# A two-layer decoder with two mixtures of experts on one core: the order of the first mixture's work, written out by hand

## The chip, the cores and the metric

One core of one Trainium2 chip runs the whole program in one launch. The metric is the device time of that launch in microseconds (us). The core has TensorE (matmul, with weight loads of its own), VectorE, ScalarE, GpSimd, and SyncE, which only issues DMAs here. Each engine has one queue that it works in order; the engines meet by semaphores alone.

## The reference, cut to what matters

The program is a decoder of six blocks over x (8 sequences of 112 tokens, 256 channels), each of them a residual block with a layer norm behind it: a linear attention, a cross attention with an MLP, a mixture of 8 experts, a second causal attention, a second cross attention, and a mixture of 4 experts. The change concerns the third block alone:

```python
capacity = max(1, int(CF * N / E))            # 896 tokens, E = 8, CF = 1.25: 140 slots for each expert
disp = zeros((E, capacity + 1, D)).at[se, pos].set(xf[st])[:, :capacity]
g = jnp.einsum('ecd,edf->ecf', disp, wg)      # D = 256, F = 1024
u = jnp.einsum('ecd,edf->ecf', disp, wu)
eo = jnp.einsum('ecf,efd->ecd', jax.nn.silu(g) * u, wd)
```

A router picks two experts for each token; a token beyond an expert's 140 slots is dropped. Every expert runs over all of its 140 slots.

## The kernel before, in words

The program is cut into seven stages (0 to 6); the stage numbered 2 is the first mixture of experts. Within a stage the builder first makes a plan, a list of units such as `("up", e, f)`, and then each engine's function (`tensor_s2`, `scalar_s2`, `vector_s2`, `gpsimd_s2`, `sync_s2`, L1275 to L1539) walks the same list and issues its own part of each unit. So the order of the plan is the order of every queue. `step(...)` tells of each unit which semaphore marks it sets, which PSUM bank it takes and who frees it, and a nominal cost. `place(unit)` appends a unit. `weave(...)` takes several generators in turn and places what they yield; `until(...)` holds a generator back until named units are placed, and `rest(ns)` until units of so much nominal cost are placed.

The units of stage 2, for expert e:

- `ein`: ScalarE issues the DMA that brings the expert's 140 rows (140 KB) from DRAM (L1347). For the first it waits for the last of the 16 scatters with which GpSimd puts the tokens into their slots (L1520, eight after each of the two `slot2`); later ones wait for the transposes of two experts before.
- `einT`, `einS`: TensorE turns the rows (four transposes, L1305); ScalarE writes the float16 high half, VectorE the low half (L1355, L1488). All products of the experts are three float16 products, high x high, high x low and low x high.
- `split(e, j, half)`, j = 0, 1, 2 for wg, wu, wd: one half of one weight (128 x 1024) is copied from float32 to float16 times 64 by ScalarE (L943), and VectorE computes the low rest from raw and high (L948). It waits for the weight's load, and, since the float16 buffers are two and the expert two before had the same one, for that expert's last up-product (wg, wu) or its down-products (wd).
- `load(e, j)`: SyncE issues the 1 MB load of expert e's weight j (L1533). There is one raw buffer for each of the three weights, so it waits for both halves of the split of expert e-1's weight j.
- `up(e, f)`, f = 0 to 7: 12 matmuls of 128 x 128 with 140 columns, gate then up. ScalarE computes silu (L1362), VectorE multiplies (L1495). `hid(e, f)`, for two f at once: ScalarE copies the product to float16 (L1369), VectorE subtracts (L1500). It waits for the gate of f+1.
- `down0(e)`, `down1(e)`: 24 matmuls with 256 columns each, for the two halves of the slots (L344 through `mm`, as all products). They need all of `hid` and of wd. VectorE then copies the result out (L1508) and SyncE stores it (L1537).

The plan before comes from four generators, `s2_down`, `s2_up`, `s2_in` and `s2_split`. What they place for a middle expert, here expert 1 with what stands around it, is:

```
up.0.7 split.2.0.0 hid.0.6 split.2.0.1 load.3.0 split.2.1.0 split.2.1.1 load.3.1
down0.0 einT.1 down1.0 einS.1 split.2.2.0 up.1.0 ein.2 split.2.2.1 up.1.1 load.3.2
up.1.2 hid.1.0 up.1.3 up.1.4 hid.1.2 up.1.5 up.1.6 hid.1.4 up.1.7 split.3.0.0 hid.1.6
```

At the head of the experts' part stand `ein.0`, the six splits of expert 1 (each pair with the load of expert 2 behind it), `einT.0`, `einS.0` and then `up.0.0`; expert 0's weights were split in stage 1. The last expert's ups are woven with the downs of the one before. The plan up to `slots2` (router, ranks, scatters) is the same before and after the change. `mx2` is a ring of the eight PSUM banks; up frees its bank with the gate, down with the copy out, einT with the low half.

Of the kernel before, what the change touches and what calls it, by code (L numbers as in the profile page):

```python
# [30 lines left out]
E0, F0, CAP = 8, 1024, int(1.25 * T_ / 8)  # L31
SLOTS = E0 * CAP
HC = CAP // 2
FT = F0 // P
# [107 lines left out]
def program(nc, a, out):  # L142
    with ExitStack() as ctx:
        build(nc, ctx, a, out)


def build(nc, ctx, a, out):
# [3 lines left out]
    def results(name, by=1):  # L151
        return Results(ctx.enter_context(nc.semaphore(name)), by)
# [10 lines left out]
    def parse(text):  # L163
        out = []
        for word in text.split(","):
            if word.strip():
                engine, name = word.split()
                out += [(engines[engine[0]], name)] if name[0] != "+" else \
                    [(engines[engine[0]], None)] * int(name)
        return out  # L170

    def step(what, marks="", bank=None, freed="", cost=0.0):

        steps[what] = (parse(marks), bank, parse(freed), cost)

    def place(unit):
        what, *at = unit
        marks, bank, freed, cost = steps[what]
        for result, name in marks:
            result.plan((name, *at) if name else None)  # L180
        if bank:
            rings[bank.replace("#", str(at[0])) if "#" in bank else bank].take(unit, *((r, (n, *at)) for r, n in freed))
        plans[-1].append(unit)
        placed.add(unit)
        spent[0] += cost
# [3 lines left out]
    def weave(*streams):  # L189
        live, passed = list(streams), 0  # L190
        while live:
            for stream in list(live):
                units = next(stream, "end")
                passed = 0 if units else passed + 1
                hurry[0] = passed >= len(live)
                assert passed <= 3 * len(live), "every stream waits for another"
                if units == "end":
                    live.remove(stream)
                    continue
                for unit in units or ():  # L200
                    place(unit)

    def until(*units):
        while any(u not in placed for u in units):
            yield None

    def rest(ns):
        end = spent[0] + ns
        yield None
        while spent[0] < end and not hurry[0]:  # L210
            yield None

    def follow(work, items):
        for i in items:
            yield from work(i)
# [10 lines left out]
    def end_stage():  # L226
        fences.append([r.planned() for r in (T, A, V, G)])
# [44 lines left out]
    eout = nc.dram_tensor("expert_out", [SLOTS, D], F32)  # L272
# [65 lines left out]
    L_eout = [results(f"dma_e_out{i}", 16) for i in range(2)]  # L338
# [33 lines left out]
    REST, REST_POWER, POWER_NS = 1500.0, 1500.0, 180.0  # L372
# [531 lines left out]
    def split_units(e, j):  # L904
        for half in range(2):
            yield [("split", e, j, half)]
# [294 lines left out]
    step("down0", "", "mx2", "V eo", 2600)  # L1201
    step("down1", "T down, V eo", cost=2600)
    step("load")

    def count_passes(b, hf):


        cut = min(max(b - 4 * hf, 0), 4) * N
        out = [(lo, hi, op) for lo, hi, op in ((0, cut, ALU.is_ge), (cut, HALF, ALU.is_gt)) if hi > lo]
        first = len(count_passes(b, 0)) if hf else 0  # L1210
        return [(*p, first + n) for n, p in enumerate(out)]
# [15 lines left out]
            L_put.plan(("put", k, b))  # L1227
    place(("slots2",))

    def s2_in(e):  # L1230
        if e >= 2:
            yield from until(("einT", e - 2))
        yield [("ein", e)]
        L_in[e % 2].plan(("ein", e))
        yield from rest(3 * REST)
        if e >= 2:
            yield from until(("up", e - 2, FT - 1))
        yield [("einT", e)]
        yield [("einS", e)]

    def s2_up(e):
        yield from until(("einS", e), ("split", e, 0, 1), ("split", e, 1, 1))
        if e >= 2:
            yield from until(("down1", e - 2))
        for f in range(FT):
            if f % 2 == 0:
                rings["silu2"].take((e, f), (V, ("hid", e, f)))
            units = [("up", e, f)]
            if f % 2 == 0 and f:
                units.append(("hid", e, f - 2))  # L1250
            yield units
        yield [("hid", e, FT - 2)]

    def s2_down(e):
        yield from until(("up", e, FT - 1), ("hid", e, FT - 2), ("split", e, 2, 1))
        yield from rest(2 * REST)
        yield [("down0", e)]
        L_eout[e % 2].plan(("eout", e))
        yield [("down1", e)]

    def s2_split(e):
        for j in range(3):
            if e >= 2:
                yield from until(("up", e - 2, FT - 1) if j < 2 else ("down1", e - 2))
            yield from split_units(e, j)
            if e + 1 < E0:
                place(("load", e + 1, j))

    weave(*(follow(w, range(E0)) for w in (s2_down, s2_up, s2_in)), follow(s2_split, range(1, E0)))
    end_stage()  # L1270

    def wide(t):
# [1673 lines left out]
```

## Time and profile before

| what | us |
|---|---|
| median of 3 runs (1519.33 to 1522.53) | 1519.48 |
| the profiled execution's own time | 1514.58 |
| its span | 1512.8 |
| TensorE matmul busy in it | 1147.1 (76%) |
| VectorE busy | 724.9 (48%) |
| ScalarE busy | 601.4 (40%) |
| GpSimd busy | 293.4 (19%) |

The busy times are sums over engines that work beside each other, so they don't add up to the span. The span is from the first to the last instruction of the profiled execution. The part of the experts lies between 406 and 556 us of it. A row of the timeline gives start, duration, engine, line, operation, the tiles written and read, and the count of merged instructions; in square brackets stands how long the engine had been idle before, and what ended that.

### The profile page before, as it was taken

The page shows a single profiled execution, that of the slowest core. Times are in us where ns is not written, and L with a number is a line of the kernel's source. Part 1 is how long each engine was busy: PE and PEld are TensorE (multiplying, and loading weights), DVE is VectorE, ACT ScalarE, POOL GpSimd, SP SyncE. Part 2 cuts the span into 40 slices and gives each one's busy share as a digit, 9 for nine tenths or more (in the row PEclk, how much of TensorE's full clock was granted, in tenths as well). Part 3 has the DMA queues.
Part 4 walks back from the last instruction along what each step waited for, and adds up shares of the span by engine and source line. Part 5 has one row for each costly group of instructions (what it writes and reads, how often), then busy time and mean ns, then how long its engine had stood idle before and what let it go on. Part 6 is the DMA issues. An engine that isn't in the chain of part 4 may idle for free.

```text
span 1512.8 us, 20695 instructions
## 1 busy us (share of the span) xinstructions
PE 1147.1 (76%) x8320; PEld 810.4 (54%) x8320; DVE 724.9 (48%) x1676; ACT 601.4 (40%) x1404; POOL 293.4 (19%) x308
## 2 busy tenths in 40 slices
PE   7987687875177755867769878878888577768996
PEld 4665465653077653545555555555556345554764
DVE  3323576216656626645433645545555355444403
ACT  4311275420145512433324533444445245447452
POOL 3311133100400024111111011001000604313353
PEclk9867699666589886788889999999999778776998
DMA  8400244004255322000005000000000000000000
GB/s 278 87 0 26 56 91 93 12 0 153 96 191 188 129 102 69 1 0 1 0 1 221 1 11 9 4 11 1 1 1 1 1 0 1 1 1 1 1 2 25
DMA packets 32752, 70.62 MB, mean 47 GB/s; under 512 B 8256, under 2 KB 22560, under 8 KB 28448
## 3 DMA queue, kind: packets, MB, share of 16 engines
q1 hardware_dynamic: 29888, 64.48, 13.9%
q0 software_dynamic: 1536, 3.67, 0.8%
q8 instruction: 65, 1.06, 0.3%
q10 hardware_dynamic: 1232, 1.15, 0.3%
q14 instruction: 31, 0.25, 0.1%
HBM read 60.19 MB, written 9.04 MB: 46 GB/s over the span
## 4 chain that ended last, share of the span: by engine, by line
PE 47%; DVE 27%; ACT 16%; POOL 4%; issue 3%; DMA 2%; SPq 0%; ACTq 0%; DVEq 0%; POOLq 0%
PE psum L344 39%; ACT s_p L2047 4%; DVE s_p L2099 3%; DVE s_k L2068 2%; POOL rs L2467 2%; DVE s_max L1115 2%; ACT sc L2347 2%; PE psum L1003 2%; DVE s_max L2088 2%; PE psum L975 1%; ACT s_k L2020 1%; DVE s_pT L2080 1%; DVE junk L1448 1%; DVE s_q L1767 1%; DVE k L2411 1%
## 5 line engine op out<-in xcount | busy, mean ns | idle before, releaser
L496 POOL TENSOR_TENSOR rstd<-meanvar,minus_half 112x1 f32<-112x1 f32 x40 | 23.2, 579 | 508.0 <-DVE meanvar L482 507.9
L2047 ACT ACTIVATE s_p<-psum,s_max 112x375 f32<-112x375 f32 x128 | 72.1, 568 | 103.6 <-DVE s_max L2088 103.6
L344 PE MATMUL psum<-ctx,Wk 128*128 128x375 f16 x320 | 64.2, 332 | 26.0 <-DVE s_k L2068 11.8
L2068 DVE SCALAR_TENSOR_TENSOR s_k<-psum,s_k 128x375 f16<-128x375 f32 x64 | 34.0, 546 | 96.8 <-ACT s_k L2020 96.8
L1115 DVE TENSOR_REDUCE s_max<-psum 112x2 f32<-112x750 f32 x64 | 59.9, 936 | 39.2 <-PE psum L975 38.4
L344 PE MATMUL psum<-wd,hid 128*70 128x256 f16 x384 | 55.8, 314 | 21.6 <-DVE hid L1500 21.6
L344 PE MATMUL psum<-x_ch,w_Wq 128*128 128x224 f32 x192 | 55.7, 421 | 14.8 <-DVE s_k L2068 8.7
L344 PE MATMUL psum<-Wv,ctx 128*125 128x512 f16 x240 | 63.3, 395 | 2.9 <-ACT s_v L2027 1.4
L456 PE MATMUL psum<-ident,x_tok 112*128 112x112 f32 x80 | 18.2, 325 | 61.0 <-DVE x_tok L491 57.6
L2088 DVE TENSOR_REDUCE s_max<-psum 112x1 f32<-112x375 f32 x128 | 63.6, 538 | 0.0
L344 PEld LDWEIGHTS psum<-wd,hid 128*70 128x70 f16 x384 | 48.7, 132 | 26.2 <-DVE hid L1500 22.9
L1067 ACT ACTIVATE s_pT<-psum 125x672 f32<-125x672 f32 x64 | 46.7, 730 | 38.7 <-PE psum L991 37.4
L1987 PE MATMUL psum<-ident,s_p 112*125 112x112 f32 x384 | 56.1, 278 | 5.0 <-DVE s_p L2099 5.0
L2777 POOL TENSOR_TENSOR hidden<-raw,hidden 128x448 f16<-128x448 f32 x44 | 46.7, 1061 | 64.2 <-ACT hidden L2660 62.5
L344 PEld LDWEIGHTS psum<-ctx,Wk 128*128 128x128 f16 x320 | 27.2, 99 | 57.8 <-DVE s_k L2068 18.6
L2347 ACT ACTIVATE sc<-psum,mx 112x112 f32<-112x112 f32 x128 | 33.9, 362 | 58.0 <-DVE mx L2420 58.0
L1987 PEld LDWEIGHTS psum<-ident,s_p 112*125 112x125 f32 x384 | 49.6, 188 | 13.1 <-DVE s_p L2099 10.0
L1998 PE MATMUL psum<-s_pT,s_v 125*64 125x112 f32 x768 | 53.2, 276 | 0.6 <-ACT s_attT L2055 0.6
L473 DVE TENSOR_TENSOR res<-res,psum 112x256 f32<-112x256 f32 x24 | 10.1, 421 | 91.0 <-PE psum L344 91.0
L344 PEld LDWEIGHTS psum<-x_ch,w_Wq 128*128 128x128 f32 x192 | 38.9, 221 | 27.2 <-DVE s_k L2068 14.5
L1979 PE MATMUL psum<-s_k,s_q 64*112 64x375 f16 x384 | 44.0, 334 | 11.8 <-ACT s_p L2047 11.7
L975 PE MATMUL psum<-s_kd,s_qd 48*112 48x375 f16 x128 | 27.2, 420 | 33.5 <-DVE s_max L1115 25.7
(352 smaller groups left out, 2818.1 us busy)
## 6 DMA issues: line engine op xcount, KB each, us to landing
raw_wg<-in_wg SPq DMA_DIRECT2D x8, 1024.0 KB, 4.9
raw_wu<-in_wu SPq DMA_DIRECT2D x8, 1024.0 KB, 6.4
raw_wd<-in_wd SPq DMA_DIRECT2D x8, 1024.0 KB, 4.9
ctx_raw<-in_ctxT SPq DMA_DIRECT2D x16, 375.0 KB, 3.5
s_kd<-k_halves SPq DMA_DIRECT2D x48, 93.8 KB, 3.8
k_halves<-s_k SPq DMA_DIRECT2D x8, 375.0 KB, 3.5
w_Wv<-in_Wv SPq DMA_DIRECT2D x2, 1024.0 KB, 9.9
w_Wo<-in_Wo SPq DMA_DIRECT2D x2, 1024.0 KB, 11.9
```

Source lines behind the costliest of these rows:

```text
L344: ins = TE.matmul(bank, left, right, start=i == 0, stop=last)
L1067: SC.activation(rings["pT1"][n], rings["t1"][unit][0:SCH, :, 0:NCH * N], ACT.Exp, scale=0.25).then_inc(*A.up("exp1", n))
L1115: VE.tensor_reduce(s1_max[b % 2][:, 2 * p:2 * p + 2], rings["s1"][unit][0:N, :, 0:S], X, ALU.max, negate=True).then_inc(*V.up("max1", n))
L1979: ins = TE.matmul(rings["s4"][(n, j)][0:N, 0:S], q[rows, p, u, cols(b % 2)], k[rows, p, v, :], start=i == 0, stop=i == 2)
L1987: ins = TE.transpose(rings["t4"][unit][0:SCH, c * N:(c + 1) * N], p[:, c * SCH:(c + 1) * SCH], ident[0:N, 0:N])
L1998: ins = TE.matmul(rings["o4"][n // 4][64 * j:64 * j + 64, p % 4 * N:(p % 4 + 1) * N], s4_v[p // 4][:, c, 2 * (p % 4) + j, :], rings["pT4"] ...
L2047: SC.activation(rings["p4"][2 * n + j], rings["s4"][(n, j)][0:N, 0:S], ACT.Exp, bias=s4_max[b % 2][:, h:h + 1], accum_out=s4_sum[b % 2][:, ...
L2068: VE.scalar_tensor_tensor(s4_k[b % 2][:, t, 1, :], rings["misc4"][unit][:, 0:S], 1 / WSCALE, s4_k[b % 2][:, t, 0, :], ALU.mult, ALU.subtra ...
L2088: VE.tensor_reduce(s4_max[b % 2][:, h:h + 1], rings["s4"][(n, j)][0:N, 0:S], X, ALU.max, negate=True).then_inc(*V.up(name, n))
L2099: VE.tensor_scalar(t, t, sums[:, j:j + 1], None, ALU.mult).then_inc(*V.up(name, n))
L2347: SC.activation(s[:, j, :], bank[:, j, :], ACT.Exp, bias=mx5[b % 2][:, 4 * g + j:4 * g + j + 1]).then_inc(*(A.up("exp5", *at) if j == 3 el ...
L2777: GP.tensor_tensor(dst[:, 1, f, :], raw_, dst[:, 0, f, :], ALU.subtract).then_inc(*G.up("ll", *at))
```

## The change: what it does

The four generators and their weave go. In their place the plan is written out in two loops. Expert 1's six splits are placed first, ahead of `ein.0`; the loads of expert 2 stay behind each pair. Then come `ein.0`, `ein.1`, `einT.0`, `einS.0`, `ein.2`, and for each expert its eight ups. Within them stand, at fixed f: the halves of the next expert's splits (`SPLITS`: wg behind f = 0 and 1, wu behind 3 and 4, wd behind 5 and 6), each second half followed by the load for the expert after; behind f = 2 the two downs of the expert before, in a row; behind f = 4 `einT` and `einS` of the next expert and the `ein` of the third from here. The last expert's downs stand at the end. Units, engines' functions, buffers and waits are as they were. For a middle expert e the order is now:

```
up.e.0 split.e+1.0.0 up.e.1 split.e+1.0.1 load.e+2.0 up.e.2 hid.e.0 down0.e-1 down1.e-1
up.e.3 split.e+1.1.0 up.e.4 hid.e.2 split.e+1.1.1 load.e+2.1 einT.e+1 einS.e+1 ein.e+3
up.e.5 split.e+1.2.0 up.e.6 hid.e.4 split.e+1.2.1 load.e+2.2 up.e.7 hid.e.6
```

```diff
--- before.py
+++ after.py
@@ -1201,6 +1201,7 @@
     step("down0", "", "mx2", "V eo", 2600)
     step("down1", "T down, V eo", cost=2600)
     step("load")
+    SPLITS = {0: (0, 0), 1: (0, 1), 3: (1, 0), 4: (1, 1), 5: (2, 0), 6: (2, 1)}
 
     def count_passes(b, hf):
 
@@ -1227,46 +1228,45 @@
             L_put.plan(("put", k, b))
     place(("slots2",))
 
-    def s2_in(e):
-        if e >= 2:
-            yield from until(("einT", e - 2))
-        yield [("ein", e)]
+    def expert_in(e):
+        place(("ein", e))
         L_in[e % 2].plan(("ein", e))
-        yield from rest(3 * REST)
-        if e >= 2:
-            yield from until(("up", e - 2, FT - 1))
-        yield [("einT", e)]
-        yield [("einS", e)]
-
-    def s2_up(e):
-        yield from until(("einS", e), ("split", e, 0, 1), ("split", e, 1, 1))
-        if e >= 2:
-            yield from until(("down1", e - 2))
+
+    def split_expert(e, j, half):
+        place(("split", e, j, half))
+        if half and e + 1 < E0:
+            place(("load", e + 1, j))
+
+    for j in range(3):
+        for half in range(2):
+            split_expert(1, j, half)
+    expert_in(0)
+    expert_in(1)
+    place(("einT", 0))
+    place(("einS", 0))
+    expert_in(2)
+    for e in range(E0):
         for f in range(FT):
             if f % 2 == 0:
                 rings["silu2"].take((e, f), (V, ("hid", e, f)))
-            units = [("up", e, f)]
+            place(("up", e, f))
             if f % 2 == 0 and f:
-                units.append(("hid", e, f - 2))
-            yield units
-        yield [("hid", e, FT - 2)]
-
-    def s2_down(e):
-        yield from until(("up", e, FT - 1), ("hid", e, FT - 2), ("split", e, 2, 1))
-        yield from rest(2 * REST)
-        yield [("down0", e)]
-        L_eout[e % 2].plan(("eout", e))
-        yield [("down1", e)]
-
-    def s2_split(e):
-        for j in range(3):
-            if e >= 2:
-                yield from until(("up", e - 2, FT - 1) if j < 2 else ("down1", e - 2))
-            yield from split_units(e, j)
-            if e + 1 < E0:
-                place(("load", e + 1, j))
-
-    weave(*(follow(w, range(E0)) for w in (s2_down, s2_up, s2_in)), follow(s2_split, range(1, E0)))
+                place(("hid", e, f - 2))
+            if f == 2 and e:
+                place(("down0", e - 1))
+                L_eout[(e - 1) % 2].plan(("eout", e - 1))
+                place(("down1", e - 1))
+            if 0 < e < E0 - 1 and f in SPLITS:
+                split_expert(e + 1, *SPLITS[f])
+            if f == 4 and e + 1 < E0:
+                place(("einT", e + 1))
+                place(("einS", e + 1))
+                if e + 3 < E0:
+                    expert_in(e + 3)
+        place(("hid", e, FT - 2))
+    place(("down0", E0 - 1))
+    L_eout[(E0 - 1) % 2].plan(("eout", E0 - 1))
+    place(("down1", E0 - 1))
     end_stage()
 
     def wide(t):
```

## Rows read from the trace of the kernel before

**Rows 1.** The page: span of the profiled execution

```profile
span 1512.8 us, 20695 instructions
```

**Rows 2.** Windows: stretch, length, busy PE, PEld, DVE, ACT, POOL, granted clock, DMA

```profile
415.50:426.07 10.57, 7.63 (x96) 7.45 (x96) 5.29 (x14) 5.88 (x15) 0.00 (x0) 0.82 0.44 176
426.07:517.83 91.76, 68.42 (x741) 63.42 (x741) 58.05 (x101) 47.26 (x96) 0.00 (x0) 0.87 0.54 188
517.83:549.66 31.83, 26.36 (x296) 25.31 (x296) 15.59 (x33) 11.26 (x30) 0.00 (x0) 0.89 0.06 15
```

**Rows 3.** Timeline, experts 1 and 2: start, duration, engine, line, operation

```profile
434.47 0.53 PE L344 MATMUL psum<-e_inT,wg 128*128 128x140 f16 x6 [1.23 <-ACT wd L943]
...
435.40 0.29 ACT L1362 ACTIVATE silu<-psum 128x140 f32<-128x140 f32 x1 [1.06 <-PE psum L344]
...
435.77 1.06 ACT L943 ACTIVATE wd<-raw_wd 128x1024 f16<-128x1024 f32 x1
...
436.86 1.23 DVE L948 SCALAR_TENSOR_TENSOR wd<-raw_wd,wd 128x1024 f16<-128x1024 f32 x1 [0.83 <-ACT wd L943]
...
439.17 0.51 DVE L1495 SCALAR_TENSOR_TENSOR silu<-psum,silu 128x140 f32<-128x140 f32 x2
...
441.00 0.27 ACT L1362 ACTIVATE silu<-psum 128x140 f32<-128x140 f32 x1
...
441.17 1.05 ACT L943 ACTIVATE wg<-raw_wg 128x1024 f16<-128x1024 f32 x1
...
443.39 0.44 DVE L1500 TENSOR_TENSOR hid<-silu,hid 128x280 f16<-128x280 f32 x1
443.75 1.22 DVE L948 SCALAR_TENSOR_TENSOR wg<-raw_wg,wg 128x1024 f16<-128x1024 f32 x1
...
443.89 5.33 PE L344 MATMUL psum<-wd,hid 128*70 128x256 f16 x24 [3.40 <-DVE hid L1500]
```

**Rows 4.** Timeline of PE: the first down-product of expert 3

```profile
481.07 4.11 PE L344 MATMUL psum<-wd,hid 128*70 128x256 f16 x24 [3.39 <-DVE hid L1500]
```

**Rows 5.** Timeline, experts 6 and 7

```profile
535.26 0.86 PE L344 MATMUL psum<-e_inT,wg 128*128 128x140 f16 x6 [2.51 <-DVE e_inT L1488]
...
539.66 2.78 PE L344 MATMUL psum<-wd,hid 128*70 128x256 f16 x24
...
542.28 0.53 PE L344 MATMUL psum<-e_inT,wg 128*128 128x140 f16 x6
...
545.63 0.53 PE L344 MATMUL psum<-e_inT,wg 128*128 128x140 f16 x6
...
547.10 0.53 PE L344 MATMUL psum<-e_inT,wg 128*128 128x140 f16 x6
...
548.35 0.30 DVE L1495 SCALAR_TENSOR_TENSOR silu<-psum,silu 128x140 f32<-128x140 f32 x1
548.69 0.44 ACT L1369 ACTIVATE hid<-silu 128x280 f16<-128x280 f32 x1 [0.37 <-DVE silu L1495]
...
549.66 5.43 PE L344 MATMUL psum<-wd,hid 128*70 128x256 f16 x48 [1.67 <-DVE hid L1500]
```

**Rows 6.** Chain that ended last, start of the experts: start, duration, what

```profile
403.78 2.55 DMA dispatched<-x_tok,put_i
406.36 0.59 ACTq L1347
...
412.72 2.27 DVE wd L948 x2
...
415.50 7.65 PE psum L344 x96
```

**Rows 7.** Timeline: expert 0's transposes

```profile
408.55 0.73 PE L1305 MATMUL psum<-ident,e_in 70*128 70x70 f32 x4 [20.98 <-DMA e_in<-dispatched]
```

**Rows 8.** The page, DMA issues: count, KB each, median us to landing

```profile
raw_wg<-in_wg SPq DMA_DIRECT2D x8, 1024.0 KB, 4.9
raw_wu<-in_wu SPq DMA_DIRECT2D x8, 1024.0 KB, 6.4
```

## The prediction, made blind

> **What bounds the kernel now.** I read the page first: the span [rows 1] and, in its slices, where the change can act at all. The diff touches only the stage of the first mixture's experts, so the sum is made there. The windows of that stage give its size [rows 2]: 10.57 us for the first expert's up-products, 91.76 us from the first down-product to the sixth (five periods of 18.35 us, one for each expert), 31.83 us for the last two. In the five periods TensorE is busy 68.42 of 91.76, VectorE 58.05, ScalarE 47.26: no engine is full, so it is a chain of waits, and the timeline shows it [rows 3]. Before each down0 TensorE waits 3.40 us for the low half of hid. That half is the last of its expert, and it stands on VectorE behind the first split of the weights that the expert after the next will use; the split's high half on ScalarE stands ahead of the last hid copy too (wg on ScalarE at 441.17, the low half of hid on VectorE only at 443.39). During the two downs that follow, ScalarE and VectorE are mostly idle, having run out of placed work; then wd's first split (released by the down) stands ahead of the first gate, and TensorE waits 1.23 us more. The third thing to see is the price of the wait itself: down0 after it takes 5.33 us for 24 matmuls at 443.89 and 4.11 at 481.07 [rows 3, 4], where the same 24 take 2.78 at 539.66 [rows 5], with no wait ahead. That is the lower of the two clock levels (1.2 GHz beside 2.4) for the most part of it. Six down0 run so, between those two durations; the middle is 4.7, or 1.9 over the warm one.
>
> The chain at the start [rows 6]: the last put lands at 406.33, ScalarE issues ein.0, and only then are expert 1's six halves copied, until 414.99, though their loads were issued at the head of the stage. The transposes of expert 0 are done at 409.3 [rows 7], but the copy of e_inT that they need stands on VectorE behind the six. up.0.0 starts at 415.50.
>
> **The start.** Expert 1's splits are now placed ahead of ein.0. ScalarE does them while VectorE still counts; VectorE does its six lows after slots2, while GpSimd puts. Six lows at 1.135 (2.27 for two [rows 6]) are 6.8 us and fit ahead of the last landing. The chain becomes: ein.0 at 406.36, transposes 408.55 to 409.28, high copy of e_inT about 0.4 and low 0.44 with 0.1 between, up.0.0 at 410.25: 5.25 earlier. New on this stretch are three 1 MB loads for expert 2, issued by SP after each pair, so some 10 us sooner and beside the puts. A load that has another beside it takes 6.4 against 4.9 [rows 8], 1.3 times. The last put (2.55) and ein.0 (2.2) stretched likewise cost 1.4; with GpSimd's own issue slightly slower I take 1.5. Bounds: 0 and 5.2 (puts and load doubled). Start: 3.75 gained.
>
> "GPSIMD Engine Reference" of the Trainium skill (Key points) says that GpSimd shares its SBUF interfaces with VectorE and contends with its instructions of two SBUF inputs, which the low copies are. No row read here has a put beside such a copy; if GpSimd stood still for all six the start would be 6.8 later and the whole gain 14.6 instead of 21.4.
>
> **Expert 0.** Its up-products take 7.65 with their tail (cold start included), 7.5 to the next start [rows 6]. Then TensorE no longer stops: up.1.0 to 1.2 follow at 0.735 for each f (545.63 to 547.10 is two [rows 5]), and the last hid half of expert 0 comes meanwhile, about 9.3 after up.0.0 (no splits stand ahead in e = 0). down0.0 starts at 9.7 against 10.57: 0.9 gained.
>
> **The period.** I walk the new order e by e, from down0(e-1) to down0(e), taking at each head of a queue whichever comes last:
> - Both downs warm, 2.62 each to the next start (539.66 to 542.28 [rows 5]): 5.24. In this time ScalarE and VectorE do the silu, gate and both halves of split (e+1, wg): 2 x 1.05 and 2 x 1.135, hidden.
> - up(e,3) is queued behind the downs; its silu starts 0.93 after it (434.47 to 435.40 [rows 3]). VectorE stands at the copy of e_out, which waits for the same downs, so it loses nothing to it.
> - silu to the high half of (e+1, wu): 0.17; high to low: 1.09 (435.77 to 436.86).
> - From here VectorE has work in a row: four lows at 1.135 = 4.54, gates 4, 5, 6 at 0.21 = 0.63 (0.51 for two), hid 0.36 twice (443.39 to 443.75) and the low of e_inT, taken as 0.43: 6.32. ScalarE's share of this (three highs, three silus, two hids, e_inT, one DMA issue) is about 5 us and stays ahead; each hid copy waits for the gate before, while a low keeps VectorE busy.
> - gate 7 to its hid copy 0.34, hid copy to down0 0.97 (548.35, 548.69, 549.66 [rows 5]).
> Sum 5.24 + 0.93 + 0.17 + 1.09 + 6.32 + 0.34 + 0.97 = 15.06, against 18.35. What hides the splits is the down pair and the fact that up 5 to 7 need only a bank of eight; if ScalarE fell behind, each low would wait as the second wd split does now (0.83 idle at 436.86 [rows 3]). Five periods: 16.45 gained.
>
> **The last two experts.** A sixth period of 15.06, then e = 7 with no splits: downs 5.24, f 3 to 6 at 0.735 = 2.94, and 2.56 from f 7 to the last down (547.10 to 549.66 [rows 5]): 10.74. Together 25.80 against 31.83: 6.03 gained.
>
> **The loads.** Each is issued after its pair: wg at about 4 us into a period, wu at 11, wd at 15, and wanted no sooner than 10 us later, for 4.9 to 6.4 us [rows 8]. Hidden. The three compete with one e_out and one ein of 140 KB. SP's queue holds the e_out store between wg's and wu's load, in the order of VectorE's work, so nothing waits behind it that is ready.
>
> Sum with a full clock: 3.75 + 0.90 + 16.45 + 6.03 = 27.1.
>
> **The clock.** In the walk TensorE is idle twice in each period. up 7 is issued 4.0 after up 3 (five f, four transposes of half of 0.73), at 9.3; up(e+1,0) needs the low of e_inT, at 10.8: about 1.4 idle. Three f later, at 13.1, it waits for hid until 15.06: 1.95 idle. Waits of 1.23 and 1.67 left the matmuls at full speed, 2.51 and 3.40 did not [rows 3, 5]. 1.95 lies between, nearer to 1.67, but it has the other wait shortly before. So I take three falls in six at 1.9: 5.7 lost. Bounds: 0, and 11.4 for six.
>
> Forecast: 27.1 - 5.7 = 21.4 us. The profiled execution is 1514.58 (span 1512.8), 4.9 below the median of the runs, 1519.48; the difference lies outside the argument, and I subtract from the median: 1498.
>
> **Rivals.**
> 1. The clock holds throughout: 27.1 gained, 1492.4. For it: 1.67 held. Against: two waits close together.
> 2. It falls before every down0: 15.7, 1503.8. For it: all six down0 after hid are slow now. Against: those waits were 3.40.
> 3. The splits aren't hidden in the up-products: in each of the four late halves VectorE waits 0.83 for ScalarE, 3.3 in a period, which is then 18.4 again. Left are 3.75 + 0.9 + (31.83 - 29.14) = 7.3: 1512. For it: each silu now stands behind a 1.05 us copy, and hid copies chain the two engines. Against: ScalarE has some 5 us of work in a stretch of 7.4.
> 4. Slower: TensorE never gets back to full speed, since it isn't busy in one piece any more. Place: the down pair, now on the path with nothing to cover it. Downs then cost 10.3 in place of 5.24 and the first up 0.7 more: a period of 20.8. It decides from 3.3 us of loss in a period. 5 x 2.45 + 8.4 (last two, 40.2) + 4.8 (expert 0's ups and three more, 11 at 1.4) - 3.75 = 22 slower: 1541. Against: TensorE is busy 11.6 of 15, more than the 68.42 of 91.76 of now, which is granted 0.87 on average [rows 2].
> 5. The change doesn't do what it says: the queues' order is the same where it counts, or another resource sets the stage. Within 0.2%: about 1519.5. Against: the waits named are all from the order of two in-order queues.
>
> **Chances.** Forecast 0.40, rival 1 0.24, rival 2 0.16, rival 3 0.12, rival 4 0.04, rival 5 0.04. What a measurement can tell from no change is 0.2%, 3 us: rivals 1 to 3 and the forecast are faster, 0.92; same 0.04; slower 0.04. The range holds the forecast with rivals 1 and 2 and the other bounds of the start: 1489 to 1509.
>
> **What would show it.** up.0.0 at about 411 to 412 instead of 415.5 (the start; below 410 or above 414 is wrong). Distance between down0s of 15 to 17 us; 18 with VectorE waiting for ScalarE in the lows is rival 3. TensorE's wait before down0 at 1.9, before up(e,0) at 1.4; a first down of 2.8 or of 4 to 5 us says whether the clock held. VectorE waiting for e_out's downs once in each period and then busy without a break. Loads all landed before their split. Wrong from the ground: a wait of TensorE for a bank, or silus that come late because ScalarE is full.

## The result, and the profile after

The changed kernel takes 1499.16 us (median of 4 runs, 1492.97 to 1504.21) against 1519.4 (4 runs, 1517.25 to 1522.53): a ratio of 0.9875, 95% interval 0.9832 to 0.9918. Timed again over six runs (experiment 10) it took 1501.28 against 1518.79, 0.9868 (0.9837 to 0.9899). By these ratios it is 19 to 20 us less. 1498 had been forecast.

The runs of one kernel spread by 5 to some 25 us, and much of that lies outside the changed part: the stretch ahead of the second eight puts ended at 395.07 in the trace of before and at 389.06 in that of after (389.1 to 400.2 over all twelve traces), and what lies behind the last down took 963.1 and 969.3. So all that follows is read from three stretches within the stage: from the first put of the second eight to up.0.0, from there to down0.0, and from down0.0 to down0.7. They don't repeat equally well. The third took 100.89 or 100.90 in five traces with the same loop; the first took 21.7 to 22.3 in six traces in which the kernel's start was the changed one; the second moves by some 0.9 with the place at which the clock rises in it.

The windows of after answer to [rows 2]; the columns are the same.

```profile
411.06:420.90 9.84, 9.84 (x136) 9.84 (x137) 4.64 (x14) 5.58 (x16) 0.00 (x0) 0.84 0.10 30
420.90:496.01 75.11, 58.54 (x744) 56.79 (x741) 56.61 (x100) 45.28 (x96) 0.00 (x0) 1.00 0.65 215
496.01:521.79 25.78, 20.80 (x256) 20.26 (x256) 15.85 (x33) 12.08 (x30) 0.00 (x0) 1.00 0.15 50
```

Five periods take 75.11 us where they took 91.76. VectorE and ScalarE do about the same work in both (100 and 101 instructions, 56.61 and 58.05 us; 96 and 96, 45.28 and 47.26 us). TensorE's busy time is 9.88 less, and that is not less work either: it has 744 matmuls where it had 741, and the granted clock is 1.00, not 0.87, from the first down to the last. The rest of the 16.65 us, 6.77, is time in which TensorE no longer stands idle (16.57 in place of 23.34). By this count more than half of what the five periods gained is the clock, and less than half is the waits themselves. That the shorter waits are what kept the clock up is borne out by experiment 5.

The timeline of after around one down shows the chain that is left (to be held against [rows 3]):

```profile
461.83 0.53 PE L344 MATMUL psum<-e_inT,wg 128*128 128x140 f16 x6 [1.55 <-DVE e_inT L1488]
...
463.51 1.22 DVE L948 SCALAR_TENSOR_TENSOR wd<-raw_wd,wd 128x1024 f16<-128x1024 f32 x1
...
464.65 0.30 DVE L1495 SCALAR_TENSOR_TENSOR silu<-psum,silu 128x140 f32<-128x140 f32 x1
464.98 0.44 ACT L1369 ACTIVATE hid<-silu 128x280 f16<-128x280 f32 x1 [1.49 <-DVE silu L1495]
...
465.45 0.45 DVE L1500 TENSOR_TENSOR hid<-silu,hid 128x280 f16<-128x280 f32 x1 [0.50 <-ACT hid L1369]
...
465.95 5.43 PE L344 MATMUL psum<-wd,hid 128*70 128x256 f16 x48 [1.76 <-DVE hid L1500]
...
471.22 0.53 PE L344 MATMUL psum<-e_inT,wg 128*128 128x140 f16 x6
...
471.49 0.69 DVE L1508 TENSOR_SCALAR e_out<-psum 70x512 f32<-70x512 f32 x1 [1.78 <-PE psum L344]
...
472.15 0.29 ACT L1362 ACTIVATE silu<-psum 128x140 f32<-128x140 f32 x1 [3.67 <-PE psum L344]
...
473.42 1.23 DVE L948 SCALAR_TENSOR_TENSOR wu<-raw_wu,wu 128x1024 f16<-128x1024 f32 x1 [0.64 <-ACT wu L943]
```

The wait of 3.40 before the down is 1.76 now, both downs follow each other at full speed (5.43 for 48), and the next down0 starts at 480.98: a period of 15.03. ScalarE is idle for 3.67 us ahead of the fourth silu and VectorE for 1.78 ahead of the e_out copy; this is where the down pair lies bare on the path.

The start looks otherwise than forecast. Here are VectorE, SyncE and GpSimd in the timeline of after, and behind them the last put from issue to release in its chain that ended last:

```profile
388.85 2.35 DVE L948 SCALAR_TENSOR_TENSOR wg<-raw_wg,wg 128x1024 f16<-128x1024 f32 x2
389.06 7.51 POOL L1520 DMA_INDIRECT dispatched<-x_tok,put_i  x1 [3.51 <-DVE w_k L1483]
391.12 2.36 DVE L948 SCALAR_TENSOR_TENSOR wu<-raw_wu,wu 128x1024 f16<-128x1024 f32 x2
391.28 0.33 SPq L1533 DMA_DIRECT2D raw_wg<-in_wg  x1
393.39 2.36 DVE L948 SCALAR_TENSOR_TENSOR wd<-raw_wd,wd 128x1024 f16<-128x1024 f32 x2
...
396.87 0.94 POOL L1520 DMA_INDIRECT dispatched<-x_tok,put_i  x1 [0.30 <-issue]
...
404.37 2.55 DMA dispatched<-x_tok,put_i
```

The first of the eight puts takes 7.51 us in place of 0.94: it starts 0.2 us after VectorE has begun the six low copies and ends 0.8 us after the last of them. The last put is issued 15.31 us after the first, not 8.71. From its issue to up.0.0 it is 6.69 us, where it was 11.72; so the reordering gave the 5.03 us that it was meant to give, and the stopped put took 6.60.

The Trainium skill ("GPSIMD Engine Reference", Key points) says that GpSimd shares its SBUF interfaces with VectorE and contends with its instructions of two SBUF inputs. The trace agrees, and shows how much it came to here: GpSimd finished no put during the six.

### The profile page after: what moved, and what is told of

It reads as the page before. It is cut to its first block, busy times and chain, and to the rows that moved or that the text cites. A ratio compares the mean times of both kernels' runs of the same rounds, so it can differ in the third digit from the quotient of the medians.

```text
span 1491.1 us, 20688 instructions
## 1 busy us (share of the span) xinstructions
PE 1137.2 (76%) x8320; PEld 801.7 (54%) x8320; DVE 723.0 (48%) x1676; ACT 600.1 (40%) x1404; POOL 300.4 (20%) x308
## 3 DMA queue, kind: packets, MB, share of 16 engines
q0 software_dynamic: 1536, 3.67, 0.8%
## 4 chain that ended last, share of the span: by engine, by line
PE 48%; DVE 27%; ACT 15%; POOL 5%; issue 3%; DMA 2%; SPq 0%; DVEq 0%; ACTq 0%; POOLq 0%
PE psum L344 39%; ACT s_p L2047 4%; DVE s_p L2099 3%; DVE s_k L2068 2%; POOL rs L2467 2%; DVE s_max L1115 2%; ACT sc L2347 2%; DVE s_max L2088 2%; PE psum L1003 2%; PE psum L975 2%; ACT s_k L2020 1%; DVE s_pT L2080 1%; DVE junk L1448 1%; DVE s_q L1767 1%; DVE wu L948 1%
## 5 line engine op out<-in xcount | busy, mean ns | idle before, releaser
L1987 PEld LDWEIGHTS psum<-ident,s_p 112*125 112x125 f32 x384 | 49.6, 188 | 13.1 <-DVE s_p L2099 10.0
L344 PE MATMUL psum<-wd,hid 128*70 128x256 f16 x384 | 43.4, 273 | 12.2 <-DVE hid L1500 12.2
L2099 DVE TENSOR_SCALAR s_p<-s_p,s_sum 112x375 f32<-112x375 f32 x128 | 51.3, 443 | 2.3
```

Source lines behind the costliest of these rows:

```text
L344: ins = TE.matmul(bank, left, right, start=i == 0, stop=last)
L1987: ins = TE.transpose(rings["t4"][unit][0:SCH, c * N:(c + 1) * N], p[:, c * SCH:(c + 1) * SCH], ident[0:N, 0:N])
L2099: VE.tensor_scalar(t, t, sums[:, j:j + 1], None, ALU.mult).then_inc(*V.up(name, n))
```

## The experiments

Each is an edit of the changed kernel, except number 4; number 10 is the changed kernel itself. Numbers 1, 5, 6, 7 and 9 were run once each. The three stretches of all of them, in us, read from the starts of the puts (L1520), of the first up and of the downs in each timeline:

| kernel | first put to up.0.0 | to down0.0 | to down0.7 | sum |
|---|---|---|---|---|
| before | 20.43 | 10.57 | 123.59 | 154.59 |
| after | 22.00 | 9.84 | 100.89 | 132.73 |
| 1 loads placed late | 22.29 | 10.18 | 100.90 | 133.37 |
| 2 ein.0 first | 20.43 | 10.46 | 100.89 | 131.78 |
| 3 splits in expert 0 | 15.77 | 14.00 | 100.93 | 130.70 |
| 4 old weave, splits first | 22.00 | 10.99 | 124.02 | 157.01 |
| 5 downs at f = 1 | 22.10 | 10.31 | 113.89 | 146.30 |
| 6 downs at f = 3 | 21.74 | 10.60 | 92.05 | 124.39 |
| 7 downs at f = 4 | 21.72 | 12.36 | 81.31 | 115.39 |
| 8 splits in expert 0, downs late in f = 4 | 15.57 | 14.25 | 81.44 | 111.26 |
| 9 one input | 18.69 | 10.77 | 100.89 | 130.35 |
| 10 changed kernel again | 22.08 | 10.78 | 100.90 | 133.76 |

**1. The loads of expert 2 later in the plan.**

```diff
-        if half and e + 1 < E0:
+        if half and 1 < e < E0 - 1:
             place(("load", e + 1, j))
...
     place(("einS", 0))
+    for j in range(3):
+        place(("load", 2, j))
```

> The changed kernel with the three loads of expert 2 placed behind einS.0 instead of beside the puts. Theory A (VectorE's copies with two SBUF inputs hold GpSimd): the first put of the second eight still lasts about 7.5 us, the time of the six low copies, and the last put is issued 15.3 us after it, as in the changed kernel. Rival B (the 1 MB loads on the same DMA engines hold it): with no load there the put lasts 0.94 us and the eight take 8.7 us, so up.0.0 comes 6.6 us sooner after the first put. The loop is unchanged under both: six periods of 15.0 us.

The put lasted 7.51 us as theory A has it (1498.16 us), but the run doesn't tell the theories apart, since the edit did not move the loads:

```profile
398.27 7.51 POOL L1522 DMA_INDIRECT dispatched<-x_tok,put_i  x1 [3.52 <-DVE w_k L1485]
400.34 2.35 DVE L948 SCALAR_TENSOR_TENSOR wu<-raw_wu,wu 128x1024 f16<-128x1024 f32 x2
400.49 0.33 SPq L1535 DMA_DIRECT2D raw_wg<-in_wg  x1
```

SyncE has nothing else in its queue there and waits only for the pair's two marks; a place further down a plan delays nothing on a queue that is empty up to it. The load still goes out 2.2 us after the put's start. The run settles nothing; experiment 9 takes its place.

**2. ein.0 ahead of the splits, as before.**

```diff
+    expert_in(0)
     for j in range(3):
         for half in range(2):
             split_expert(1, j, half)
-    expert_in(0)
```

> The changed kernel with ein.0 placed ahead of expert 1's six splits, as the kernel before had it; the loop stays as changed. Both theories: puts at 0.94 us each, eight of them in 8.7 us, since the low copies then come after the last put has landed; up.0.0 20.4 us after the first put of the second eight (22.0 in the changed kernel, 20.4 in the kernel before). The time is 1.6 us under the changed kernel's if the start's reordering was a loss, and 5 us over it if it was the gain that the prediction had. Loop: down0.0 to down0.7 100.9 us as in the changed kernel, 22.7 less than before; so some 22 to 23 us faster than the kernel before.

```profile
393.55 0.94 POOL L1520 DMA_INDIRECT dispatched<-x_tok,put_i  x1 [3.54 <-DVE w_k L1483]
```

The puts are 0.94 us each again and up.0.0 comes after 20.43 us, to the hundredth what it was before the change. The loop's 100.89 stays. 1494.29 us (4 runs), a ratio to before of 0.9837 (0.9793 to 0.9881). Against the changed kernel the trace gives 1.57 us less at the start and, with the clock rising later in expert 0's ups, 0.95 less in all; the runs can't tell the two apart. So the rewritten loop is the whole gain, and the new start has no part in it.

**3. Expert 1's splits within expert 0's ups.**

```diff
-    for j in range(3):
-        for half in range(2):
-            split_expert(1, j, half)
     expert_in(0)
...
-            if 0 < e < E0 - 1 and f in SPLITS:
+            if e < E0 - 1 and f in SPLITS:
```

> The changed kernel with expert 1's splits taken out of the head and placed within expert 0's ups, at the same f as for every other expert. Theory A: nothing holds GpSimd, the puts take 8.7 us, and up.0.0 starts 15.2 us after the first of them (22.0 in the changed kernel). Expert 0's ups then carry six splits: down0.0 comes 13.1 us after up.0.0 instead of 9.8. Together 3.5 us faster than the changed kernel. Rival: VectorE and ScalarE are late in expert 0 by more than that (no down pair hides wg's split) and the 6.8 us are given back: no change.

15.77 to up.0.0 and 14.00 to down0.0, against 15.2 and 13.1 expected: 2.0 us less than the changed kernel by the trace, not 3.5, and too little for the runs to tell (1497.57 us, 4 runs; 0.9868 of before, 0.9821 to 0.9914). With no low copy beside them the puts take 0.94 us each. The splits cost 4.2 us in expert 0's ups, where they are no longer hidden, of the 6.2 that the start gains.

**4. The kernel before with the new start alone.**

```diff
-    weave(*(follow(w, range(E0)) for w in (s2_down, s2_up, s2_in)), follow(s2_split, range(1, E0)))
+    for j in range(3):
+        for half in range(2):
+            place(("split", 1, j, half))
+        place(("load", 2, j))
+    weave(*(follow(w, range(E0)) for w in (s2_down, s2_up, s2_in)), follow(s2_split, range(2, E0)))
```

> The kernel before with one part of the change alone: expert 1's six splits (and the loads of expert 2 behind each pair) ahead of ein.0; the weave stays for all the rest. Theory A (low copies hold GpSimd): the first put of the second eight lasts 7.5 us, up.0.0 22.0 us after it instead of 20.4; 1 to 2 us slower than the kernel before, or not to be told from it. The prediction's own term: up.0.0 16.7 us after the first put, 3.75 us faster. Five periods of 18.35 us in both.

```profile
400.20 7.50 POOL L1524 DMA_INDIRECT dispatched<-x_tok,put_i  x1 [3.55 <-DVE w_k L1487]
408.01 0.94 POOL L1524 DMA_INDIRECT dispatched<-x_tok,put_i  x1 [0.30 <-issue]
```

Up.0.0 after 22.00 us, 1.57 later than before; the runs say 1.0037 (1526.2 us, 10 runs; 1.0000 to 1.0073), slower if anything. The term for the start had the wrong sign.

**9. What holds the put.** In the changed kernel the six low copies of expert 1 are replaced by six reductions, each over the same 1024 raw elements and nothing else. The low halves of expert 1's weights are set to zero behind einS.0 (three memsets, left out of the lines below), so that part of the computation is missing. It is placed here because it belongs to the start.

```diff
+        if e == 1:
+            n = src.shape[1]
+            VE.tensor_reduce(hid0[1][:, 0, 2 * j + half, 0:n], src, X, ALU.max).then_inc(*V.up("lo", e, j, half))
+            return
         VE.scalar_tensor_tensor(lo, src, WSCALE, hi, ALU.mult,
                                 ALU.subtract).then_inc(*V.up("lo", e, j, half))
```

> The changed kernel, but VectorE's six low copies for expert 1 are replaced by six reductions over the same raw halves, which read one SBUF tensor of 1024 elements instead of two and take about as long; the lows of expert 1 are set to zero later (so that part of the computation is left out). Theory A (it is the second SBUF input that holds GpSimd): the puts last 0.94 us each although VectorE is as busy beside them; last put issued 8.7 us after the first of the second eight, up.0.0 after 15.4 to 15.8 instead of 22.0. Rival B (VectorE working without a break holds GpSimd, whatever it reads): the first put still lasts as long as the six, 7 us.

VectorE and SyncE first, then GpSimd, then the last put from issue to release:

```profile
394.64 2.34 DVE L950 TENSOR_REDUCE hid<-raw_wg 128x1 f16<-128x1024 f32 x2
396.89 2.34 DVE L950 TENSOR_REDUCE hid<-raw_wu 128x1 f16<-128x1024 f32 x2
397.06 0.33 SPq L1540 DMA_DIRECT2D raw_wg<-in_wg  x1
399.15 2.34 DVE L950 TENSOR_REDUCE hid<-raw_wd 128x4 f16<-128x1024 f32 x2
```

```profile
394.85 0.94 POOL L1527 DMA_INDIRECT dispatched<-x_tok,put_i  x1 [3.54 <-DVE w_k L1487]
396.09 0.94 POOL L1527 DMA_INDIRECT dispatched<-x_tok,put_i  x1 [0.30 <-issue]
397.34 0.94 POOL L1527 DMA_INDIRECT dispatched<-x_tok,put_i  x1 [0.30 <-issue]
```

```profile
403.57 5.78 DMA dispatched<-x_tok,put_i
```

VectorE is as busy (7 us in a row), the loads go out beside the puts at the same distance (2.2 us after the first), and GpSimd issues every put in 0.94 us. So neither the loads nor a busy VectorE hold GpSimd; the low copies do. They differ from the reductions in two ways: they read a second SBUF tensor, and they write 1024 elements where the reduction writes a few. This run doesn't tell which of the two holds GpSimd.

The other half of the expectation failed: up.0.0 came after 18.69 us, not 15.5 (1497.28 us). Without the stop the last put is issued 2.0 us after the last of the three loads, and it takes 5.8 us to its release instead of 2.55. That is the collision which the prediction priced at 1.4 for the put and ein.0 together; here it is 3.2 for the put alone. The loads are the likely cause (in experiment 3, with none of them there, the last put takes 2.56), but no run has the reductions without the loads.

**5. The downs one f earlier.** (`if f == 2 and e:` becomes `if f == 1 and e:`.)

> The changed kernel with the two downs of the expert before behind f = 1 instead of f = 2: TensorE has 0.73 us less to do ahead of them and waits 2.5 us for hid where it waited 1.76. Theory A (a wait of 1.76 is short enough, one of 2.5 is not, as at 535.26 in the kernel before): the clock falls, the first down lasts 4 us or more in most of the six, and the period is 15.8 plus 1.5 to 1.9, about 17.4. Rival B (the clock holds because TensorE is fuller over the whole period): downs of 2.7 us each, a period of 15.8, which is the 0.73 of the up-product that now stands behind the downs and nothing else.

```profile
438.44 5.43 PE L344 MATMUL psum<-wd,hid 128*70 128x256 f16 x48 [2.49 <-DVE hid L1500]
454.20 7.10 PE L344 MATMUL psum<-wd,hid 128*70 128x256 f16 x48 [2.49 <-DVE hid L1500]
471.63 7.10 PE L344 MATMUL psum<-wd,hid 128*70 128x256 f16 x48 [2.49 <-DVE hid L1500]
```

(1507.98 us.) The first wait of 2.49 left the clock at its upper level, five further ones (2.49 and 2.50) did not: 7.10, 7.10, 7.07, 6.91 and 6.82 us for 48 matmuls. Two periods of 15.8 and then four of 17.2 to 17.4: theory A, with its number. 0.73 us of waiting more costs 1.4 to 1.67 us of slow matmuls besides. The wait before the ups is 1.55 as in the changed kernel, so the wait before the down is the only one that grew. Against this stand 37 waits of 1.76 or 1.77 before a down in six executions (after and experiments 1, 2, 3, 9, 10), and behind none of them a slow one.

That holds for this loop and is not a rule on the length of a wait. In a later stage of the kernel before, TensorE waited 1.88 us after a busy stretch at full clock, and half a microsecond after it went on, the clock fell. The windows (columns of [rows 2]) stand behind the row:

```profile
913.36 1.42 PE L344 MATMUL psum<-x_ch,w_Wq 128*128 128x224 f32 x4 [1.88 <-DVE s_k L2068]
...
909.00:911.40 2.40, 2.40 (x17) 1.47 (x16) 2.36 (x7) 0.64 (x2) 0.00 (x0) 1.00 0.00 0
914.30:915.00 0.70, 0.70 (x6) 0.29 (x6) 0.00 (x0) 0.19 (x1) 0.00 (x0) 0.50 0.00 0
```

**6 and 7. The downs later.** (`f == 3` and `f == 4` in the same line.)

> The changed kernel with the downs behind f = 3. Theory A (the period is the downs, then what VectorE has left behind the e_out copy, then gate 7 to hid to down): the first up behind the downs no longer has a silu and a split's high half in front of VectorE, which goes on at once: 5.24 + 0.2 + 0.69 (e_out) + four lows 4.54 + e_inT 0.43 + three gates 0.63 + two hids 0.72 + 0.34 + 0.97 = 13.8 us instead of 15.0. TensorE waits 1.0 before the down. Rival B (ScalarE sets the second half): still 15.0.

> The changed kernel with the downs behind f = 4 (ahead of the second half of wu's split). Theory A: one low, one gate and one hid fewer stand behind the e_out copy: 5.24 + 0.2 + 0.69 + 3.41 + 0.43 + 0.63 + 0.36 + 0.34 + 0.97 = 12.3 us in each period, six of them 16 us less than in the changed kernel. Rival B (TensorE or the banks set it): no less than 13.8.

```profile
454.89 5.43 PE L344 MATMUL psum<-wd,hid 128*70 128x256 f16 x48 [1.03 <-DVE hid L1500]
...
468.57 5.43 PE L344 MATMUL psum<-wd,hid 128*70 128x256 f16 x48 [1.02 <-DVE hid L1500]
```

```profile
453.63 5.43 PE L344 MATMUL psum<-wd,hid 128*70 128x256 f16 x48 [0.29 <-DVE hid L1500]
...
465.66 5.43 PE L344 MATMUL psum<-wd,hid 128*70 128x256 f16 x48 [0.29 <-DVE hid L1500]
```

The first two rows are of experiment 6, the others of experiment 7. The periods are 13.68 and 12.03 us, against 13.8 and 12.3 by the sum. The runs gave 1492.13 and 1480.99 us; the three stretches together are 8.3 and 17.3 us less than in the changed kernel (down0.0 itself, behind one and two further ups, comes 0.8 and 2.5 later). Whatever VectorE can do during the downs must stand ahead of the e_out copy in its queue. From experiment 6 to 7 one low, one gate and one hid went from behind it to ahead of it, 1.70 us of VectorE's work, and 1.65 came off the period.

**8. The edit of experiment 3, and the downs behind all of f = 4.** The lines show what is added; left out are experiment 3's lines and the block `if f == 2 and e:`, which is taken away.

```diff
                 if e + 3 < E0:
                     expert_in(e + 3)
+            if f == 4 and e:
+                place(("down0", e - 1))
+                L_eout[(e - 1) % 2].plan(("eout", e - 1))
+                place(("down1", e - 1))
```

> Two edits together: expert 1's splits within expert 0's ups (2 us gained in an earlier run) and the downs behind everything that f = 4 places (wu's second half, einT, einS). Theory A: behind the e_out copy stand two lows, two or three gates and a hid, 5.24 + 0.2 + 0.69 + 2.27 + 0.63 + 0.36 + 0.34 + 0.97 = 10.7, so that TensorE's own 11.4 us (16 x 0.367 + 5.24 + 0.25) or VectorE's own work (six lows 6.8, eight gates 1.7, four hids 1.5, e_inT 0.4, e_out 0.6: 11.0, plus its 0.5 wait for the last hid copy) sets the period: 11.5 to 12.3 us. The whole is some 20 us faster than the changed kernel, 40 faster than the one before. Rival B: the chain through hid stays, 13 us or more.

1479.71 us (4 runs, 1472.54 to 1488.93), 0.9748 of the kernel before (0.9685 to 0.9811), and by the trace 21.5 us less than the changed kernel. Four periods of it, in the columns of [rows 2]:

```profile
447.52:495.62 48.10, 45.95 (x589) 45.30 (x589) 44.26 (x81) 36.91 (x78) 0.00 (x0) 1.00 0.70 236
```

The period is 12.02, as in experiment 7: the late place gained nothing more. TensorE is busy 96% and VectorE 92% of it, where they had been 75% and 63%; there is little left to hide on either. A wait of 0.48 for hid still stands before the down, so which of the two sets the period was not tried.

**10. The changed kernel again.**

> The changed kernel once more, for the size of the whole and for the clock over another execution. By the trace's sum it is 21.9 us faster than the kernel before, a ratio of 0.9856. No down after the wait of 1.76 us is slow in the six periods of 15.0 us (theory: that wait is short enough wherever the clock's turns fall); the prediction had three of six slow.

100.90 for the loop, no slow down, 0.9868. Its sum of three stretches is 20.8 less than before, not 21.9; up.0.0 to down0.0 took 10.78 here and 9.84 in the first trace. The difference is the clock: expert 0's matmuls came to full speed 5.4 us after up.0.0 here and 3.4 us after it there.

## Why the prediction was right, and where it was right by luck

The time came out 1.2 us from the forecast, yet two of its terms were wrong by more than 5 us, with opposite signs, and they cancelled. The loop was right by its working; the total was right by luck.

| step | forecast gain | in the trace of after |
|---|---|---|
| start | 3.75 | -1.57 |
| expert 0 | 0.90 | 0.73 |
| five periods | 16.45 | 16.65 |
| last two experts | 6.03 | 6.05 |
| clock | -5.7 | 0 |
| sum | 21.4 | 21.86 |

(The rows of measured gain hold the clock's share already, so its own row is the slow matmuls that were expected and didn't come.)

- **The period** was forecast at 15.06 and is 15.02 or 15.03 in every trace with this loop (the first of a trace 15.00). Its structure held too: the down pair on the path, VectorE waiting 1.78 us at e_out for the same downs, then four lows with their gates and hids in a row. Experiments 6 and 7 move it by what the same sum says, to 0.3 us, so the chain is shown, not only fitted. What the splits needed was a place at which VectorE had nothing to do.
- **The last two experts** came as the sum had them. **Expert 0** did in this trace, in which the clock rose as late after up.0.0 as in that of before (3.4 us). In experiments 1, 2 and 10, with the same plan from up.0.0 on, it rose 4.1 to 5.4 us after it, and the stretch took 10.18 to 10.78 against 10.57: where the clock rises is worth as much as the term.
- **The start** failed at the step "VectorE does its six lows after slots2, while GpSimd puts". They don't run beside the puts, they stretch the first of them to 7.5 us (experiments 2, 4 and 9). The prediction had worked this out as 6.8 us and given it no chance of its own, because no row showed the pair; it is 6.60. The other part of the term was right: 5.25 forecast, 5.03 measured. The term for the loads, 1.5, came to nothing here, since the last put, now 6.6 us late, took 2.55 as before; in experiment 9, where it fell beside them, it was too small (3.2 for the put alone). Its factor 1.3 had little under it: 4.9 and 6.4 are the medians for wg and wu, and the profile's page has 4.9 again for wd.
- **The clock** failed as a middle taken between a wait of 1.67 that held and one of 2.51 that did not. The wait was 1.76, not 1.95: the next expert's up.0 started 10.9 us into the period, not 10.8, its three ups ended at 13.26, not 13.1, and the down came at 15.02, not 15.06. At 1.76 the clock holds in this loop: 37 times in 37. At 2.49 it falls five times in six (experiment 5). The fear that two waits shortly after one another add up (1.55 before the ups, 1.76 before the down) was not borne out. What a fall costs was sized a little high, 1.9 against 1.4 to 1.67.
- **The rivals.** Rival 1, the clock holding throughout, is what happened in the loop; its total, 1492.4, missed by what the start lost. Rival 2, a fall before every down, is what experiment 5 came to, for five downs of six. Rival 3 (low copies waiting for ScalarE, 0.83 each) is not there: 0.64 at the first wu copy, which the walk holds in its 0.17 and 1.09, and 0.46 at the first wg copy, beside the downs. Rivals 4 and 5 have nothing in the trace.

What stays open: the sum of the stretches gives 21 to 22 us, the runs 19.0 and 20.0 with intervals of 5 to 7 us to either side. They agree; but with one trace of the kernel before it can't be said whether the stages that the change doesn't touch became 1 or 2 us slower by it. What lies behind the last down took 963.1 us in that trace and 964.7 to 973.6 in the others, but 971.7 also in experiment 4, whose loop is the old one. And whether it is the second input or the long output of the low copy that stops GpSimd was not tried.

## What to carry to other kernels

In a plan shared by in-order queues, look for the engine that carries most of the period's work and for the instruction in its queue that waits for a long block elsewhere: what stands ahead of it is hidden by the block, what stands behind it is on the path. Move work across that line until the engines' own sums are near the period (here 18.35, 15.0, 13.7, 12.0 us for the same instructions). A wait on TensorE has two prices, its length and the clock, and here the second was the larger (9.9 of 16.65 us in five periods): keep waits below those behind which the same loop's traces show slow matmuls, and look at the granted clock again after each change. And work put into an idle stretch of one engine isn't free if it stops the engine that is on the path, as six copies of VectorE stopped a put of GpSimd; look for a row in which the two run side by side before counting on it.

## What the runs showed that I had not expected

- One GpSimd put beside six VectorE copies with two SBUF inputs, run without a break, lasted 7.51 us instead of 0.94 (six further executions with the same overlap: 7.50 or 7.51). With six one-input reductions of the same length: 0.94.
- With three 1 MB loads issued in the 6.5 us before it, the last put took 5.8 us from issue to release, and 2.55 without them.
- In this loop a wait of 1.76 us on TensorE before the downs never lowered the granted clock, and one of 2.49 did in five cases of six.
